# Graph convolutions of a four-layer network: node update in the gather stage, in units of four blocks

## The reference

```python
def _graph_conv(h, src, dst, Wr, br, Ws, ew=None):
    m = h[src]
    if ew is not None:
        m = m * ew[:, None]
    agg = jax.ops.segment_sum(m, dst, num_segments=h.shape[0])
    return agg @ Wr + br + h @ Ws
h = relu(_graph_conv(x, src, dst, Wr0, br0, Ws0, edge_weight))
h = relu(_graph_conv(h, src, dst, Wr1, br1, Ws1))
x = layernorm(x + h)
```

## Time and profile before

| what | value |
|---|---|
| median of three runs | 9079.56 us (9075.75 to 9084.97) |
| span of the profiled execution, slowest core (the page gives no other time of it) | 9077.3 us |
| busy: PE, DVE, ACT, POOL | 61%, 56%, 25%, 68% |
| first gather of the last layer's two convolutions issued | 6696.7 us and 7875.1 us |
| mean granted TensorE clock | 0.665 |

### The profile page before, as it was taken

How to read it: one execution, slowest core, us unless ns; L and a number is a source line. 1 busy time by engine, 2 the same in 40 slices (tenths; PEclk the granted TensorE clock), 3 DMA queues, 4 the chain that set the end, 5 groups by cost and what they waited for, 6 DMA issues and landing times. The chain is left out here.

```text
span 9077.3 us, 124550 instructions
## 1 busy us (share of the span) xinstructions
PE 5529.8 (61%) x32289; PEld 4875.7 (54%) x32289; DVE 5121.2 (56%) x14751; ACT 2279.7 (25%) x4226; POOL 6148.2 (68%) x6249
## 2 busy tenths in 40 slices
PE   6777757777639997036777755777733333433334
PEld 5666657777627775026676645666623333333333
DVE  7777654444489997045777743445554444444445
ACT  0111111111127775023444433444320000000000
POOL 2777767777627777747777727777537777577774
PEclk9556558888757776567888865555555555655556
DMA  1000007777627765025555533444312222221111
GB/s 33 13 12 12 10 11 211 210 210 210 179 55 162 163 163 115 2 64 141 139 139 137 130 38 79 80 80 81 58 39 53 53 53 53 50 52 52 52 52 47
DMA packets 993339, 792.54 MB, mean 87 GB/s; under 512 B 426646, under 2 KB 868378, under 8 KB 992720
## 3 DMA queue, kind: packets, MB, share of 16 engines
q1 hardware_dynamic: 536692, 373.45, 17.0%
q0 software_dynamic: 211680, 354.89, 16.1%
q10 hardware_dynamic: 244600, 60.13, 3.0%
HBM read 693.22 MB, written 94.60 MB: 87 GB/s over the span
## 5 line engine op out<-in xcount | busy, mean ns | idle before, releaser
L1426 PE MATMUL sum_ps_sum<-sum_hot,sum_msg 128*128 128x128 f32 x3528 | 841.2, 431 | 1420.1 <-DVE acc L1395 1362.7
L1426 PEld LDWEIGHTS sum_ps_sum<-sum_hot,sum_msg 128*128 128x128 f32 x3528 | 770.7, 330 | 1490.7 <-DVE acc L1395 1421.5
L514 POOL DMA_INDIRECT payload_src<-load_src_pay_slot,load_src_at_i x882 | 873.2, 990 | 439.7 <-issue 270.1
L641 POOL DMA_INDIRECT payload_dst<-place_dst_pay,place_dst_at_i x882 | 926.2, 1050 | 352.4 <-issue 304.5
L1370 POOL DMA_INDIRECT sum_rows<-x_table,dst_other x882 | 844.4, 957 | 442.5 <-issue 268.5
L1370 POOL DMA_INDIRECT sum_rows<-conv_table,dst_other x882 | 843.9, 957 | 334.0 <-issue 268.5
L1495 POOL DMA_INDIRECT attend_rows<-xl_table,dst_other x882 | 867.9, 984 | 295.7 <-issue 267.3
L1495 POOL DMA_INDIRECT attend_rows<-h_table,dst_other x882 | 858.0, 973 | 303.3 <-issue 268.3
L1045 POOL DMA_INDIRECT scores_rows<-kv_table,scores_idx x882 | 834.4, 946 | 308.5 <-issue 248.1
L1568 PE MATMUL attend_ps_sum<-attend_hot,attend_msg 128*128 128x128 f32 x3528 | 690.8, 366 | 372.7 <-DVE acc L1730 327.0
L1555 PE MATMUL attend_ps_x<-attend_win,attend_hot_t 128*128 128x136 f32 (+1 forms) x3528 | 770.9, 327 | 228.1 <-DMA attend_rows<-xl_table,dst_other 166.3
(11 more groups left out here) (437 smaller groups left out, 13710.0 us busy)
## 6 DMA issues: line engine op xcount, KB each, us to landing
attend_win<-xr_table SPq DMA_DIRECT2D x882, 68.0 KB
scores_win<-q_table ACTq DMA_DIRECT2D x882, 64.0 KB
spill<-scores_rows SPq DMA_DIRECT2D x126, 448.0 KB
place_dst_key_all<-key_rows_dst SPq DMA_DIRECT2D x126, 448.0 KB
place_dst_rows<-spill SPq DMA_DIRECT2D x126, 448.0 KB
attend_rel_all<-rel_flat_dst SPq DMA_DIRECT2D x252, 224.0 KB
place_dst_low_all<-low_rows_dst SPq DMA_DIRECT2D x126, 224.0 KB
payload_src<-load_src_pay_slot,load_src_at_i POOLq DMA_INDIRECT x882
```

Of the source, the lines that this page charges most:

```text
L514: pool.indirect_dma_start(o.payload, bass.IndirectOffsetOnAxis(ap=at_i[:, s, j:j + 1].bitcast(U32), axis=0), pay_slot[:, s, j, :], None).t ...
L641: pool.indirect_dma_start(o.payload, bass.IndirectOffsetOnAxis(ap=at_i[:, t:t + 1].bitcast(U32), axis=0), pay[:, t, :], None).then_inc(sca ...
L1426: mm = pe.matmul(ps_sum[:, n, j, :], msg[:, n, j, :], hot[:, n, j, :], start=True, stop=True)
```

## The change

`gather_sum` and `node_update` become one stage, `gather_conv`. Its loops over groups are written out, 126 times each on PE, DVE and ACT; the semaphores are waited for at constants. The 50 blocks are 13 units of four (the last of two).

The own-row part runs beside every ninth of the first groups: PE turns a unit's own rows, ACT copies them, PE multiplies them by `ws` and adds the bias by a product with a row of ones, ACT copies the result to `nodes`.

The rest of a unit comes one iteration after the group in which its last edge can lie at the latest. PE multiplies both halves of the sums by `wr` into one PSUM place, straight from `acc` and `odd`, so the join is left out. DVE adds the own-row part. In the first convolution ACT rectifies in place and SP stores. In the second, DVE also rectifies and adds the residual in one operation and makes the statistics and the shift; ACT makes the root and the normalization; SP stores.

```diff
--- before.py
+++ after.py
-def gather_sum(nc, c, o, name, acc, alpha, table, unit=None, deep=9, near=3):
+def gather_conv(nc, c, o, name, acc, alpha, table, k, unit=None, deep=9, near=3):
+    own, nodes, last = k["own"], k["nodes"], k.get("residual") is not None
+    UB = 4
+    units = [(u, min(u + UB, NB)) for u in range(0, NB, UB)]
+    NU = len(units)
+    tile_of_end = lambda node: (E + N - (N - 1 - min(node, N - 1)) - 1) // P
+    settled = [tile_of_end(b1 * P - 1) // G for _, b1 in units]
+    tail_units = lambda g: [u for u in range(NU) if settled[u] == g]
+    make_at = [9 * u for u in range(NU)]
...
+        ps_sum, ps_n = st.ps("sum", [P, near, 8, P]), st.ps("n", [P, 2, UB, P])
...
+            @block.scalar
+                def take_turned(u):
+                    act.wait_ge(turned, u + 1)
+                    if u:
+                        act.wait_ge(produced, u)
+                    act.copy(xt[:, 0:size(u)], ps_n[:, 0, 0:size(u)]).then_inc(xt_ready, 1)
+                def take_base(u):
+                    act.wait_ge(produced, u + 1)
+                    act.copy(of(nodes, u), ps_n[:, 1, 0:size(u)]).then_inc(base_ready, 1)
+                def rectify(u):
+                    act.wait_ge(taken, u + 1)
+                    act.activation(of(nodes, u), of(nodes, u), ACT.Relu).then_inc(rectified, 1)
+                def normalize(u):
+                    act.wait_ge(var_ready, u + 1)
...
+                    act.activation(rs[:, u % 2, 0:size(u)], inverse[:, u % 2, 0:size(u)], ACT.Sqrt).then_inc(rs_ready, 1)
+                    act.wait_ge(shift_ready, u + 1)
...
+                    for q in range(size(u)):
+                        act.activation(z[:, u % 2, q, :], h[:, u % 2, q, :], ACT.Identity, bias=shift[:, u % 2, q:q + 1],
+                                       scale=rs[:, u % 2, q:q + 1]).then_inc(normed, 1)
+                for g in range(R + 2):
+                    if g in make_at:
+                        take_turned(make_at.index(g))
+                    if g - 2 in make_at:
+                        take_base(make_at.index(g - 2))
...
+                    for u in tail_units(g - 1):
+                        (normalize if last else rectify)(u)
...
+            @block.sync
+                for u in range(NU):
+                    if last:
+                        sp.wait_ge(normed, units[u][1])
+                        sp.dma_start(rows_of(k["out"], u), z[:, u % 2, 0:size(u)]).then_inc(z_free[u % 2], 16)
+                    else:
+                        sp.wait_ge(rectified, u + 1)
+                        sp.dma_start(rows_of(k["table"], u), of(nodes, u)).then_inc(stored, 16)
...
             @block.vector
+                def take_sum(u):
+                    dve.wait_ge(multiplied, u + 1)
...
+                    if last:
...
+                        dve.tensor_tensor(hu, made, base, ALU.add).then_inc(taken, 1)
+                        dve.wait_ge(taken, u + 1)
+                        link(dve.scalar_tensor_tensor(hu, hu, 0.0, of(k["residual"], u), ALU.max, ALU.add))
...
+                        link(dve.tensor_scalar(ve[:, u % 2, 0:size(u)], mv[:, u % 2, 0:size(u), 1], LN_EPS, None, ALU.add))
...
+                        dve.reciprocal(inverse[:, u % 2, 0:size(u)], ve[:, u % 2, 0:size(u)]).then_inc(var_ready, 1)
+                        dve.wait_ge(rs_ready, u + 1)
+                        dve.scalar_tensor_tensor(shift[:, u % 2, 0:size(u)], mv[:, u % 2, 0:size(u), 0], -1.0,
+                                                 rs[:, u % 2, 0:size(u)], ALU.mult, ALU.mult).then_inc(shift_ready, 1)
+                        dve.wait_ge(shift_ready, u + 1)
+                    else:
+                        dve.tensor_tensor(base, made, base, ALU.add).then_inc(taken, 1)
...
-                with dve.Fori(0, R // deep - 1) as i:
...
-                dve.tensor_tensor(acc[:], acc[:], odd[:], ALU.add).then_inc(joined, 1)
-                dve.wait_ge(joined, 1)
+                message(0)
+                for g in range(R + 1):
+                    if g + 1 < R:
+                        message(g + 1)
+                    if g < R:
+                        add(g)
+                    for u in tail_units(g - 1):
+                        take_sum(u)
+                dve.wait_ge(taken, NU)
...
             @block.tensor
+                def turn_own(u):
...
+                    for q in range(size(u)):
+                        mm = pe.transpose(ps_n[:, 0, q, :], own[:, units[u][0] + q, :], c.ident[:])
+                def own_products(u):
...
+                    for q in range(size(u)):
+                        pe.matmul(ps_n[:, 1, q, :], xt[:, q, :], k["ws"], start=True, stop=False)
+                        mm = pe.matmul(ps_n[:, 1, q, :], c.ones[0:1, :], k["b"], start=False, stop=True)
+                def sum_products(u):
+                    pe.wait_ge(added, 2 + G * (settled[u] + 1))
+                    if u < 2:
+                        pe.wait_ge(xt_ready, NU)
+                        pe.wait_ge(base_ready, NU)
+                    else:
+                        pe.wait_ge(taken, u - 1)
+                    for q in range(size(u)):
+                        b = units[u][0] + q
+                        pe.matmul(ps_n[:, u % 2, q, :], acc[:, b * P:(b + 1) * P], k["wr"], start=True, stop=False)
+                        mm = pe.matmul(ps_n[:, u % 2, q, :], odd[:, b * P:(b + 1) * P], k["wr"], start=False, stop=True)
+                    mm.then_inc(multiplied, 1)
+                for g in range(R + 1):
+                    if g < R:
+                        sums(g)
+                    if g in make_at:
+                        turn_own(make_at.index(g))
+                    if g - 1 in make_at:
+                        own_products(make_at.index(g - 1))
+                    for u in tail_units(g - 1):
+                        sum_products(u)
...
-        gather_sum(nc, c, by_dst, "sum3", acc, by_dst.weight, x_table, unit)
-        node_update(nc, c, "conv0", acc, x, "conv",
...
-        gather_sum(nc, c, by_dst, "sum4", acc, unit, conv_table)
-        node_update(nc, c, "conv1", acc, x, "last",
...
+        gather_conv(nc, c, by_dst, "conv0", acc, by_dst.weight, x_table,
+                    {"own": x, "wr": conv_w[:, 0], "ws": conv_w[:, 1], "b": conv_b[0:1, 0], "nodes": h_nodes,
+                     "table": conv_table}, unit)
+        gather_conv(nc, c, by_dst, "conv1", acc, unit, conv_table,
+                    {"own": h_nodes, "wr": conv_w[:, 2], "ws": conv_w[:, 3], "b": conv_b[0:1, 1], "nodes": h_nodes,
+                     "residual": x, "out": out})
```

255 lines of the change are left out of this document (75 added, 180 removed).

## The result

| | before | after |
|---|---|---|
| median (four runs each), us | 9082.26 (9075.75 to 9086.20) | 9005.51 (9002.13 to 9008.12) |
| ratio after / before | | 0.9917 [0.9905, 0.9928] |
| span of the profiled execution, us | 9077.3 | 9001.3 (own time 9003.18) |

A forecast was written before the change was run, and what follows sets the result against it. POOL's gathers were taken as the bound, at 8.74 us a group, with the work after each last gather bare. Gains of 43.1 and 53.5 us sum to 96.6: 9079.6 - 96.6 = 8983 us, range 8970 to 9003.

The forecast's parts named there:

- The bound before: Both gather stages: POOL's gathers set the pace for 125 groups; what follows the last gather is bare.
- First convolution, -43.1: After its last gather: PE's trailing products are late next; second stage starts at 7832.0 instead of 7875.10, gaining 43.1 us.
- Second convolution, -53.5: Its tail: DVE becomes the bound from group 120 on; end at 9023.8 instead of 9077.3, gaining 53.5 us.
- DVE's 64.0 us: Second convolution's tail: DVE's summed work from the message of group 121 until 9018.1, without waiting for rows.
- the unit of 3.55: Second convolution: DVE's 3.55 us per four-block unit for add, statistics, root wait, shift and rectify-and-residual pass.
- Rival 1: Second convolution's unit is cheap, 2.8 us; DVE hardly lags; 8974 us; chance 0.08.
- Rival 2: Both convolutions: products and DVE take turns, DVE waiting 3.6 us for each unit's eight products; 9049 us; chance 0.06.
- The own-row part, 0: Groups 0 to 110: own-row transposes and products fit in PE's slack, ACT is empty there; cost 0.
- Also at 0: the loops written out: Group loops: constants replace register arithmetic and a gather doesn't depend on them; cost 0.
- The rule: Gathers beside DVE: two SBUF inputs hold the shared ports, so gathers lack descriptors; weighed as contradicted by the one-hots' pace.
- Rival 3: Second convolution's new pass reads two SBUF operands and stops POOL while it runs; +2 us, 8985; chance 0.02.
- Rival 4: Every group of both stages: written-out DVE and PE streams stall for their own instructions; slower, 9147 us; chance 0.03.

The follow-up runs named there:

- e15: Kernel after with groups 9 to 107 of DVE and PE in a loop of nine again; 9004.73 us, ratio to before 0.9903.
- e13: Kernel before with the loop of gather_sum written out on DVE alone, PE still looped; 9141.53 us, ratio 1.0051.
- e3: Kernel before with only the groups' loops of gather_sum written out on DVE and PE; 9117.30 us, ratio 1.0016.
- e14: Kernel before with the loop of gather_sum written out on PE alone, DVE still looped; 9089.76 us, ratio 1.0000.
- e2: Kernel after, unchanged, profiled once more; 9024.25 us once.
- e4: Kernel after with a tiny DVE fill between the wait for a group's rows and its message; 9016.68 us, ratio to before 0.9905.
- e17: Kernel after, unchanged, timed on another chip (before 9110.00 us there); 9079.16 us, ratio 0.9965.
- e1: Kernel before, unchanged, profiled once more; 9087.59 us once.
- e16: Kernel before with one DRAM array longer by 128 rows that nothing reads or writes; 9095.41 us, ratio 1.0004.
- e18: Kernel after with groups 9 to 107 looped on DVE and PE, accumulators filled and messages made by ACT; 9084.63 us, ratio to before 0.9972.

## Why the prediction came out as it did

- **The bound before**: right. Two stages paced by POOL, and what follows the last gather bare.
- **First convolution, -43.1**: measured -43.7. Last gather to last message 5.6 us instead of 4.3, last message to next stage 17.1 instead of 19.0: two misses that partly cancel, so the sum is nearer than its terms. I had PE start the trailing products at 1.2 GHz and rise 6 us into its work. The first trailing product starts at 7837.30, and from 7838.55 on they follow each other every 0.22 us, which is the step of the 2.4 GHz stretch in the earlier trace rows; the granted clock from 7828 to 7850 is 0.82 in the mean.
- **Second convolution, -53.5**: measured -57.1. DVE's 64.0 us came as 64.6 and the unit of 3.55 as 3.61, so Rival 1 (2.8) and Rival 2 (turns with PE) are out: DVE waits there 3.5 us for ACT's root, which the 3.55 held, once 0.8 us for itself, and never for PE. The rest is small: DVE's unbroken stretch begins 34.8 us ahead of the last gather instead of 32.5 (8967.7 - 8932.88; 8986.6 - 8954.11), and the end comes 2.9 us after the last compute, not 4.8.
- **The own-row part, 0**: nothing in the runs speaks against it; its products lie in the gather stages (PE 492 us busy against 417), and all of DVE's idle time ahead of the first convolution's messages, 653.3 us, is ended by rows. It wasn't tried alone.
- **The step that failed** is "Also at 0: the loops written out (constants replace register arithmetic; a gather doesn't depend on them)", with its premise that both stages keep 8.74 us a group. A gather does depend on DVE's stream, through the phase. The two stages lost 4.6 and 6.1 us, all of it held gathers. e15 shows within one execution that the written-out messages do it (16 of 54 hold a gather, none of 198 looped ones). The size isn't a property of the edit: DVE's stream alone costs 48.5 us in the two stages of e13, and DVE's and PE's together 5.8 us in e3 on another chip. Whether the constant wait or the constant operands bring the message forward wasn't separated.
- **The second term that failed** is larger and wasn't written down: the sum gives nothing to the stages ahead of the change, and they took 14.1 us more. Either loss alone would have left the time inside my range; that both came, and that this chip put the phase where it cost 10.7 and not 48 us, is chance.
- **The rule** that I weighed for this, the second half of the Trainium skill's "SBUF: two separate sides" ("SBUF — State Buffer"), was right: it tells what holds a gather. I dismissed it because the pace beside the one-hots was kept in the mean; I should have asked whether any gather beside one was long. The mean of 957 ns over a median of 944 was the trace: 882 x 13 ns = 11.5 us, 7.4 of it in one gather and the rest in 17. Rival 3 had the mechanism with the wrong place: in the profile after one gather begins in the new pass and takes 0.99 us; the message and the one-hot, which were there before, carry the price.
- **Rival 4** (slower, 9147) had the right edit and a wrong price and mechanism: the issue time is 268.4 or 268.5 us in both stages of before, after, e13 and e14.
- **Not foreseen and not settled**: the untouched attention stages. The second took 1136.5 to 1147.7 us in the six 9.0 to 9.1 ms profiles with DVE's stream written out (after, e2, e3, e4, e13, e17) and 1125.7 to 1134.6 in the five with loops (before, e1, e14, e15, e16), but 1142.3 in e18, which has loops. The time is in held gathers again, and the phase moves there too: in the first attention stage its median is -0.06 to -0.05 us in the six profiles with loops, e18 included, and -0.02 to +0.03 in the six without. Why a stream that comes later in the program does that to a stage with the same code isn't shown. The whole time is that of before in e14 and e16 (ratios 1.0000 and 1.0004), so neither PE's stream nor the array's place is seen to do it, though the kernel before wasn't profiled on their chip. What gives each chip its own place for the phase isn't shown either; the kernel before had medians of 9082, 9091, 9103 and 9110 us in four sets of runs and 11502 and 11659 on two other chips.

No version run beats the kernel after beyond its interval; the lowest ratios are e15's 0.9903 and e4's 0.9905.

## What to carry to other kernels

Units of an update that are settled early can be taken between the last groups, and the gain can be worked out to a few microseconds from the rows of an earlier layer. But the pace of the engine that sets it isn't a constant of the edit: look at the distribution of its instruction, not the mean, find what the long ones begin beside, and put a range on every step that moves that neighbour by even 0.1 us, a loop written out with constant waits included. Measure such a change on more than one chip: the changed kernel was faster on each on which it was timed, by 0.35% to 0.83%.

## What the runs showed of the hardware

- A gather that begins while DVE runs an operation with two SBUF inputs ends 0.81 to 0.83 us behind that operation, up to 1.87 us instead of 0.944. With one input in PSUM none of 152 was held in two stages, against 208 of 211 with both in SBUF.
- Which of the two gives way is decided at 0.044 us: 442 gathers that began up to 0.044 us after a message weren't touched, 188 that began 0.044 to 0.11 us after one were held. Where the gather isn't held and begins between 0.03 us before and 0.044 us after the message, the message is the longer one, up to 1.17 us instead of 1.09 (8932.88 above has 1.16). So a shift of some hundredths of a microsecond changes a price of 0.07 us on DVE, which has slack, into 0.9 us on POOL, which has none.
- The 8.3 us gather isn't fully explained. It begins between the records of DVE's two fills and ends 0.81 us behind the one-hot that follows the second (after):
```profile
7850.84 5.39 DVE L1503 MEMSET acc<- 128x6400 f32 x1 [6.08 <-issue]
...
7855.06 0.94 POOL L1426 DMA_INDIRECT conv_rows<-conv_table,dst_other  x1 [0.30 <-issue]
...
7856.31 8.35 POOL L1426 DMA_INDIRECT conv_rows<-conv_table,dst_other  x1 [0.30 <-issue]
7857.52 5.39 DVE L1503 MEMSET conv_odd<- 128x6400 f32 x1 [1.28 <-issue]
...
7862.82 1.03 DVE L1454 TENSOR_TENSOR conv_hot<-const_column,dst_rel 128x896 f32<-128x896 f32 x1
```
  Gathers that begin in the first fill take 0.94 us, so a fill alone doesn't hold one as a message does. With ACT's fills, 5.5 us each, the long gather is gone.
